# Running an image's opening one loop pass ahead, with its pair products, in a two-image pipeline on one core

## The reference

```
h = layernorm(x)*(1+ca)+sa ; x = x + ga * scan_block(h)        # a: in-projection, conv, silu, step sizes,
                                                                #    16-state selective scan over 256 tokens, out-projection
h = layernorm(x)*(1+cb)+sb ; x = x + gb * routed_block(h)      # b: 8 experts, top 2, plus a shared one
h = layernorm(x)*(1+ca1)+sa1; x = x + ga1 * delta_block(h)     # c: 8 heads, conv on q, k, v, gated delta rule
h = layernorm(x)*(1+cb1)+sb1; x = x + gb1 * attention_moe(h)   # d: attention, then 8 softly gated experts
```

## Time and profile before

| what | value |
|---|---|
| median of three runs | 2813.85 us (2810.82 to 2817.66) |
| span of the profiled execution | 2813.2 us |
| one pass of the loop | 166.7 to 171.2 us, by the start of the first `c_prod` on VectorE |
| busy share of the span: PE, DVE, ACT, POOL | 87%, 79%, 43%, 20% |
| granted TensorE clock, mean over the span | 0.938 of 2.4 GHz |

### The profile page before, as it was taken

The page is one execution under the profiler, slowest core; times in us unless marked ns, Lnnn a source line. Parts: engine busy times, 40 slices in busy tenths (PEclk is TensorE's granted clock), DMA queues, the critical chain, the costliest instruction groups (busy, mean ns, idle before and its releaser), DMA issues.

```text
span 2813.2 us, 61085 instructions
## 1 busy us (share of the span) xinstructions
PE 2441.0 (87%) x22584; PEld 1893.0 (67%) x22584; DVE 2212.7 (79%) x5136; ACT 1200.1 (43%) x2697; POOL 549.1 (20%) x497
## 2 busy tenths in 40 slices
PE   3688989888898988989888898988989889898997
PEld 2466768667686766768667586766758667686776
DVE  6677897878879887787878879887887978879742
ACT  3332536344353543436444353543536444253512
POOL 2122221122222022121112222022121112222010
PEclk7789999999999999999999999999999999999998
DMA  4000000000000000000000000000000000000000
GB/s 132 4 2 3 7 4 1 8 3 8 3 7 2 3 8 3 7 3 4 5 3 8 3 7 2 3 8 3 7 3 5 4 3 8 3 7 2 1 6 3
DMA packets 24835, 21.46 MB, mean 8 GB/s; under 512 B 7218, under 2 KB 21571, under 8 KB 24531
## 3 DMA queue, kind: packets, MB, share of 16 engines
q1 hardware_dynamic: 24530, 17.26, 2.2%
HBM read 15.13 MB, written 2.13 MB: 6 GB/s over the span
## 4 chain that ended last, share of the span: by engine, by line
PE 32%; issue 32%; DVE 27%; POOL 4%; ACT 2%; DVEq 0%; POOLq 0%; ACTq 0%
DVE wide L1382 4%; DVE wide L1394 3%; PE banks L891 3%; PE banks L1198 3%; PE banks L1024 3%; PE banks L1188 3%; DVE wide L1402 3%; PE banks L1016 2%; PE banks L1052 2%; DVE inv L1570 2%; PE banks L1005 2%; DVE inv L1566 2%; PE banks L963 1%; PE banks L1065 1%; DVE inv L1557 1%
## 5 line engine op out<-in xcount | busy, mean ns | idle before, releaser
L1519 DVE SCALAR_TENSOR_TENSOR wide<-pad,conv,wide 128x256 f32<-128x256 f32 x864 | 370.0, 496 | 0.0
L561 POOL TENSOR_TENSOR wide<-wide 128x512 f32<-128x512 f32 x128 | 188.3, 1471 | 832.0 <-DVE wide L1402 472.0
L1394 DVE TENSOR_TENSOR_SCAN wide<-wide 128x1024 f32<-128x1024 f32 x128 | 292.9, 2288 | 1.9 <-ACT wide L667 0.3
L667 ACT ACTIVATE wide<-small,a_neg 128x255 f32<-128x255 f32 x512 | 216.0, 496 | 173.9 <-DVE wide L1394 173.0
L1044 PE MATMUL banks<-hideb,identb 128*128 128x512 bf16 x800 | 272.1, 403 | 0.0
L1188 PE MATMUL banks<-inv,up 128*128 128x256 f32 x1024 | 264.5, 387 | 0.0
L1198 PE MATMUL banks<-down,inv 128*128 128x128 f32 x2048 | 256.5, 276 | 0.0
L1198 PEld LDWEIGHTS banks<-down,inv 128*128 128x128 f32 x2048 | 248.7, 192 | 5.0
L796 ACT ACTIVATE inv<-banks,up1b 128x256 f32<-128x256 f32 x512 | 214.0, 480 | 52.0 <-PE banks L1188 51.5
L1024 PEld LDWEIGHTS banks<-inv,mats 64*64 64x64 f32 x5120 | 168.3, 139 | 63.9 <-issue 62.1
L1024 PEld LDWEIGHTS banks<-inv 64*64 64x64 f32 x5120 | 159.5, 135 | 67.4 <-issue 65.3
(11 more groups left out here) (280 smaller groups left out, 4933.4 us busy)
## 6 DMA issues: line engine op xcount, KB each, us to landing
gates_bc<-gate_rows SPq DMA_DIRECT2D x32, 128.0 KB, 2.9
x<-in_x SPq DMA_DIRECT2D x16, 128.0 KB, 2.1
up<-in_W SPq DMA_DIRECT2D x1, 2048.0 KB
out<-xn_y SPq DMA_DIRECT2D x16, 128.0 KB, 2.1
wide<-in_wmod SPq DMA_DIRECT2D x2, 384.0 KB, 5.6
con<-in_con SPq DMA_DIRECT2D x1, 724.0 KB, 4.7
w_k<-in_Wk SPq DMA_DIRECT2D x1, 512.0 KB
w_q<-in_Wq SPq DMA_DIRECT2D x1, 512.0 KB
```

Source lines behind the costliest of these rows:

```text
L561: g.tensor_tensor(ypart[p % 2], r[:, 0:512], r[:, 512:1024], ALU.add).then_inc(a_yp.h, 1)
L667: last = s.activation(decay[st % 2][:, at + 1:at + T], dt[:, c, 1:T], ACT.Exp, scale=a_neg[:, c, st * SG + q:st * SG + q + 1])
L1394: v.tensor_tensor_scan(state[st % 2], decay[st % 2], drive[st % 2], 0.0, ALU.mult, ALU.add).then_inc(a_h.h, 1)
L1519: v.scalar_tensor_tensor(dst, src, w, dst, ALU.mult, ALU.add).then_inc(c_conv.h, 1)
```

## The change

There are three parts instead of two. `OPEN` (letter w) is the opening and runs for image i+1; x, without its opening and with `PAIRS` at its end, runs for image i; y, now from `INVERT` on, for image i-1. `follow` writes turn(-1) with w, turn(0) with w and x, a loop of 14 turns with all three, a turn with x and y, and one with y.

The opening works in one bank, 5: the in-projection's second half waits until ScalarE has copied the first half out, B, C and rank wait until z is used, and the step sizes follow in the same bank. It has norm tiles of its own (`stats_w`, `mv_w`, `xn_w`, `hT_w`). `c_logd` moves to bank 2 and `c_prod` to banks 0 and 1, so the first scan step of the next image waits for the last `c_prod`, and the first `lev_TT` waits for the step sizes of the next image. The zeroing of the decays moves from `a_norm` to the first scan step on GpSimd. Some semaphores are merged, waits for earlier images are spelled out, the strings in `TURNS` are new, and `WARM` has 36 dummy matmuls per pass instead of 50.

```diff
+OPEN = [("a_norm",), ("a_norm2",), ("a_turn",), ("a_in",), ("a_conv",), ("a_zgate",), ("a_silu",), ("a_silu2",),
         ("a_xproj",), ("a_dt",), ("a_split",), ("a_soft",), ("a_step",)]
+SCAN = []
...
-FIRST_HALF = SCAN + ROUTED + PROJECT
-SECOND_HALF = PAIRS + INVERT + APPLY + ATTEND + EXPERTS
+FIRST_HALF = SCAN + ROUTED + PROJECT + PAIRS
+SECOND_HALF = INVERT + APPLY + ATTEND + EXPERTS
+PARTS = (("w", OPEN, 1), ("x", FIRST_HALF, 0), ("y", SECOND_HALF, -1))
...
     "gpsimd": (
-        "yyxxyyyyyyxxxxxxxyxyxxyyxyxxx"),
+        "xxxxxxxxxyxyxyyxyxwxxxxxxxxxx"),
...
+            turn(-1, "w")
+            turn(0, "wx")
+            with eng.Fori(1, NB - 1) as i:
+                turn(i, "wxy")
+            turn(NB - 1, "xy")
+            turn(NB, "y")
...
             def a_in(i):
                 t.wait_ge(ln_h[0].h, ln_h[0].at(i, 1))
...
-                    last = t.matmul(bank(1, T, c * T), w_in[:, c * P:(c + 1) * P], hx[:], start=True, stop=True)
+                    last = t.matmul(bank(OPEN_BANK, T, c * T), w_in[:, c * P:(c + 1) * P], hw[:], start=True, stop=True)
                 last.then_inc(a_xi.h, 1)
+                t.wait_ge(a_pad.h, a_pad.at(i, 1))
...
             def a_xproj(i):
-                keep_warm(0, "a_xproj")
+                t.wait_ge(a_zs.h, a_zs.at(i, 1))
...
                 if st == 0:
                     t.wait_ge(a_split.h, a_split.at(i, 6))
-                    t.wait_ge(a_vb.h, a_vb.at(i, 2))
-                    t.wait_ge(a_zs.h, a_zs.at(i, 1))
+                    if not is_first(i):
+
+                        t.wait_ge(c_AT.h, c_AT.at(i - 1, 2 * GROUPS))
...
-                t.matmul(bank(5), con[:, C_GT:C_GT + P], gmask[gr % 2].rearrange("p h t -> p (h t)"), start=True, stop=False)
-                t.matmul(bank(5), identb[:], hideb[:].unsqueeze(1).broadcast_to([P, HG, P]), start=False, stop=True).then_inc(c_D.h, 1)
+                else:
+                    t.wait_ge(c_ss.h, c_ss.at(i, 1))
+                t.matmul(bank(2), con[:, C_GT:C_GT + P], gmask[gr % 2].rearrange("p h t -> p (h t)"), start=True, stop=False)
+                t.matmul(bank(2), identb[:], hideb[:].unsqueeze(1).broadcast_to([P, HG, P]), start=False, stop=True).then_inc(c_D.h, 1)
```

More of the change, by code:

```diff
@@ L448, in follow, with turn @@
         def follow(eng, turns, steps):
-            first = [step for step in FIRST_HALF if step[0] in steps]
-            second = [step for step in SECOND_HALF if step[0] in steps]
-            for name, *args in first:
-                steps[name](0, *args)
-            with eng.Fori(1, NB) as i:
-                at = {"x": 0, "y": 0}
-                for half in turns:
-                    name, *args = (first if half == "x" else second)[at[half]]
-                    at[half] += 1
-                    steps[name](i if half == "x" else i - 1, *args)
-            assert at == {"x": len(first), "y": len(second)}
-            for name, *args in second:
-                steps[name](NB - 1, *args)
+            mine = {part: [step for step in order if step[0] in steps] for part, order, _ in PARTS}
+            ahead = {part: n for part, _, n in PARTS}
+            assert all(turns.count(part) == len(mine[part]) for part in mine)
+            def turn(i, parts):
+                at = dict.fromkeys(mine, 0)
+                for part in turns:
+                    name, *args = mine[part][at[part]]
+                    at[part] += 1
+                    if part in parts:
+                        steps[name](i + ahead[part], *args)
+            turn(-1, "w")
[4 more added lines that the diff above has]
+            turn(NB, "y")
         @block.sync
@@ L694, in c_proj @@
                 at = m
[L695 removed]
+                if m == 0 and is_first(i):
                     s.wait_ge(loaded_late, LOADED_LATE)
@@ L816, in _ @@
             for n, (l, part) in enumerate(((0, 2), (0, 5), (1, 2), (1, 5))):
-                last = t.matmul(PS[0:NB, 5, n * D:(n + 1) * D], cT[:, l, :], wmod[:, l, part * D:(part + 1) * D], start=True, stop=True)
+                last = t.matmul(PS[0:NB, 6, n * D:(n + 1) * D], cT[:, l, :], wmod[:, l, part * D:(part + 1) * D], start=True, stop=True)
             last.then_inc(mod_done, 1)
@@ L859, in a_dt_ @@
                 t.wait_ge(a_bc.h, a_bc.at(i, 2))
-                t.wait_ge(a_pad.h, a_pad.at(i, 1))
                 for c in range(CB):
-                    last = t.matmul(bank(1, T, c * T), w_dt[:, c * P:(c + 1) * P], rank_sb[:], start=True, stop=True)
+                    last = t.matmul(bank(OPEN_BANK, T, c * T), w_dt[:, c * P:(c + 1) * P], rank_sb[:], start=True, stop=True)
                 last.then_inc(a_dtp.h, 1)
@@ L1034, in lev_TT @@
                 keep_warm(7, "lev_TT", l, ch)
+                if l == 0 and ch == 0 and not is_last(i):
+                    t.wait_ge(a_vb.h, a_vb.at(i + 1, 2))
                 t.wait_ge(c_W.h, c_W.at(i, l * TILES + ch + 1))
@@ L1502, in c_proj @@
                     n = m - 3
-                    if n == 0 and not isinstance(i, int):
+                    if n == 0 and not is_first(i):
                         v.wait_ge(c_rms.h, c_rms.at(i - 1, 8))
```

154 lines of the change are left out of this document (82 added, 72 removed).

## The result

The changed kernel takes 2846.18 us (median of 4 runs, 2841.6 to 2848.16) against 2815.76 us of the kernel before (4 runs, 2810.82 to 2823.88): a ratio of 1.011, 95% interval 1.0085 to 1.0135. It is slower by 1.1%, where 0.7% faster was forecast. The profiled execution has a span of 2843.0 us, so 29.8 us more than before. First the page's first part, columns as in the earlier trace rows.

What follows compares the result with a forecast made beforehand. VectorE was taken to bound front, scan stage and convolutions, TensorE the tail. Per pass 41.8 + 32.4 + 36.75 + 55.2 = 166.15 against 167.5, −1.35; over 15 passes −20, from 2813.2 to 2793 us; range 2735 to 2848.

Steps and rivals of the forecast that it cites:

- the scan stage's sum: Scan stage: 5.2 us of turns and maskings plus 0.7 raise it from 49.3 to 55.2 us.
- Their rounds on PE and one more hand-over: 0.7: Scan stage: TensorE rounds of the four turns and maskings moved there, plus one hand-over, add 0.7 us.
- TensorE's clock: Rival: pauses around pair products and first inversion rounds lower TensorE's clock, 3.4 us more a pass, 2844 us; chance 0.26.
- The sign that the prediction named for it: Granted clock from first pair product to first drive: 0.95 or more expected, near 0.8 if the clock's case came.
- Tail and front: Last convolution to first drive: the rebuilt chain takes 36.75 us instead of 45.6, so 8.85 less.
- The branch: VectorE's loop branch, now between last pair product and the mask needing it, costs 2.8 us on the path.
- the products: Pair products on VectorE: 14.55 us together, including a 3.0 us wait for ScalarE's second exponential behind two table loads.
- The step to the first product: From the last convolution until the first pair product can start, through VectorE, GpSimd's roots and mask, and TensorE: 15.3 us.
- Convolutions: Convolution stage: the opening's normalising adds 0.7 us and waits for ScalarE's copy 0.9, so 30.8 becomes 32.4.
- Middle: Middle stage: stays at 41.8 us, bounds −0.9 (residual fits beside waits) to +1.6 (q, k, v and scores ahead of `b_out`).
- The rival of hidden waits: Rival in tail and front: branch (2.8 us) or ScalarE's loads (3.0) are off the path; either alone about 2749 us; chance 0.22.
- The double price of the loads: Rival in the pair products: each of two ScalarE table loads costs another 1.28 us, wait 5.6, time 2832; chance 0.03.

Runs made afterwards that it cites:

- the run without dummies: The changed kernel with the fourteen dummy matmuls of its scan stage taken out: 2846.23 us, ratio 1.0113.
- the run on the expert's block: The changed kernel with TensorE's second matmul block of expert 6 moved behind the first group's pair products: 2840.85 us, ratio 1.0086.
- that kernel's own dummies: The kernel before, with more dummy matmuls in its own pauses: 2803.23 us, ratio 0.9971.
- the run with dummies alone: The changed kernel with added dummy matmuls in scan stage and middle, no order changed: 2780.47 us, ratio 0.9891.
- the same two mends: On the changed kernel, VectorE's loop branch moved behind the delta block's scales (2843.95 us), and a new ScalarE and VectorE order in the pair products (2832.98 us).

## Why the prediction was wrong, step by step

**The step that failed is the scan stage's sum,** "Their rounds on PE and one more hand-over: 0.7", and with it the chance given to the clock. The work was right: 5.2 us of turns and maskings were forecast, and the stage has 52 us of VectorE in it against 46.5 in the earlier trace rows. What failed is the price of the rounds. They were priced at full clock, but the granted level falls about the pauses ahead of them (2.6 us at TensorE's branch, 5.1 until the first drive, 2 between rounds), and the rounds are waited for. The sum had the clock at nothing, in this stage and in the middle.

That the clock is the cause, and not a mark of it, is shown by the dummies: they add no result and change no order, and brought the ratio from 1.011 to 0.998 (scan stage) and then to 0.989 (middle as well). The scan stage fell from 59.1 to 56.4 us, so the clock made 2.7 of the 3.9 us by which it missed 55.2. The other 1.2 stay at full clock: VectorE's waits for the rounds are 39.8 us there for 26.8 before, 0.9 a pass, and what the dummies themselves cost is not known. The changed kernel's own twelve passes follow 55.4 us + 0.38 for each us at the lower level, which would make 3.7; but they lie between 4.4 and 14.3 us of it, and the run without dummies left that line. The middle fell from 42.9 to 41.0, by 2.0 (its twelve passes follow 40.3 + 0.30 for each, with 8.5 us at that level).

**The rival "TensorE's clock"** named this mechanism and gave 2844 us, 0.1% from the result, with a chance of 0.26 against 0.38. What spoke for it was in the earlier trace rows: both stages with pauses had a fallen clock. What I held against it, that half of the work is covered by VectorE, holds for the front, where 5.6 us at the lower level cost little, but not for the scan stage, where VectorE waits for each round. Its place was also wrong: the first products ran at full clock, the inversion did not. The sign that the prediction named for it, the clock from the first product to the first drive, read 0.91 in the pass shown, but the time was lost elsewhere. So its figure is partly luck: it had 3.4 us a pass at the pair products, and the dummies gave back 2.7 in the scan stage and 2.0 in the middle.

**Tail and front:** the products (14.9 for 14.55), the wait for ScalarE (3.00 for 3.0) and the mask with its turn (4.06 for 4.1) were right. The branch came along as forecast, 2.2 for 2.8, and the runs in which it moved show that it is a cost of the branch itself, as the rule of the Trainium skill had it (Runtime: NRT & Kernel Launch, section Instruction fetch mechanics): it left the mask with the branch, and 17.5 us of the time with it where the clock was held. That the wait is for a fetch of instructions is that section's account; no row here shows it. The step to the first product was too short, 15.3 for 17.7. TensorE came to the first sum 15.5 us after the opening's convolution, where the forecast had 6.1 + 6.8 + 0.6 = 13.5, though TensorE itself was on time: from the third norm's turn to that sum it took 53.3 us, and the forecast's terms give 48.5 − 1.9 + 5 + 1 + 1.5 = 54.1. It is VectorE's convolutions that ended 2.6 us earlier than forecast, so that the step is counted from an earlier start. VectorE's own chain is as late, by the 4.46 us of waiting for B, C and rank. In the run on the expert's block, 2.03 us went out of TensorE's queue between those and the sum, and only 0.8 came through, as the wait stayed. Taking B and C earlier in TensorE's order was not run.

**Convolutions:** forecast +1.6, measured −1.0. The 0.9 us of waits for ScalarE did not come (VectorE is busy for 29.80 of 29.80 us), and the last product (0.69 us) now stands behind the opening's convolution, so that it counts in the next stage. With TensorE as the bound this gained nothing: convolutions and step to the first product together are 29.8 + 17.7 = 47.5 us, and 32.4 + 15.3 = 47.7 by the forecast.

**Middle:** forecast 0 within −0.9 to +1.6, measured +1.2 at a fallen clock. At full clock it is 41.0 for 41.8 before (41.4 with that kernel's own dummies), inside the bounds. That q, k, v and the scores ahead of `b_out` would cost is not borne out: the run that put them behind it lost 7.7 us a pass, 4.6 of them at full clock. Whether q, k and v two blocks earlier, as before, would gain is not shown.

**The rival of hidden waits** (branch and loads off the path) is out: both waits stand in the trace. The double price of the loads is out as well.

**Cancelling errors.** At full clock the pass is 166.1 us by the run with dummies alone, and 166.15 by the forecast. That agreement is partly luck. The convolutions' −2.6 and the +2.4 to the first product are one shift, as said above, and cancel by the mechanism. The rest does so by chance: +1.2 in the scan stage (56.4 for 55.2), −0.8 in the middle, −0.6 at the branch and +0.3 in the products. And 166.15 was set against the example pass of 167.5, not the mean of 168.2: against the mean, 15 × 2.05 = 31 us less is 2782, near the 2780 of that run, where the forecast had 2793.

**What stays open** is why the fourteen dummies that were taken out cost nothing, how the loss is shared among the rounds of the scan stage, and how the 1.2 us that it keeps at full clock divide between the rounds and the dummies.

## What to carry to other kernels

When a change puts two engines' work in one chain, price each of its matmul rounds at both clock levels, by rows of the trace at either, and look for the pauses ahead of it: a stage that is sized at full clock is right only if something keeps TensorE busy there. A mend that shortens a pause's neighbour may show no gain while the clock is free to fall elsewhere, so hold the clock first (dummy matmuls in the pauses that end on the path) and then judge orders and waits; here the same two mends gave nothing and 0.5% when each was alone (ratios 1.0112 and 1.0060 for 1.011), and 1.8% together behind it (0.9891 to 0.9711). Lay a loop's branch where its engine waits anyway.

## What the runs showed of the hardware that was not expected

The time at the lower clock did not come at random: in the changed kernel the lengths of the passes repeated in fours (about 170.5, 172, 172.4 and 168 us, by the starts of the first product), and in the run with VectorE's branch moved all twelve passes had one length, 170.5 to 170.7 us, with 9.5 us at the lower level in the scan stage and 13.7 in the middle each time. There the 1.6 us saved in tail and front were thus paid back in full in the middle. Dummy matmuls of 512 columns in a row took 0.23 us each at full clock, so a pause of 5 us needs twenty. And a round of 64 matmuls of 64x64 took 2.08 us at full clock and 3.53 to 3.68 at the lower, some 1.7 times as long, not twice. Nor is that because part of such a round lies at full clock: halves of rounds (32 matmuls) that lie wholly at the lower level take 1.97 us in the median, those wholly at full clock 1.15.
